# TensorE's wait for the scaled key copies moved from ahead of the key-key products to between them and the key-query products

## What is computed

```
qkvz = x @ W_qkvz.T                       # per key head: q, k, 2 v, 2 z of 128
q, k, v = silu(conv4(q)), silu(conv4(k)), silu(conv4(v))
q, k = rmsnorm(q), rmsnorm(k)             # sums of squares of q and k
decay[c, m] = exp(g[c] - g[m])            # c >= m, g a running sum
T = inverse(I + strict_lower(beta * (k k^T) * decay))
attn = (q k^T) * decay                    # key-query products
for each chunk:                           # the state carries over
    v_new = T (beta v) - T (beta k exp(g)) state
    out = (q exp(g)) state + attn v_new
    state = state * exp(g_last) + (k * exp(g_last - g))^T v_new
out = rmsnorm(out) * silu(z) @ W_out.T
```

## Time and profile before

| what | value |
|---|---|
| median of 3 runs | 3789.3 us |
| the profiled execution | 3785.71 us, its span 3783.8 us |
| TensorE matmul busy | 88% of the span |
| TensorE weight load busy | 69% |
| VectorE, ScalarE, GpSimd busy | 65%, 52%, 40% |
| mean granted TensorE clock | 0.982 |

### The profile page before, as it was taken

How to read it: one execution, slowest core, us unless ns; L and a number is a source line. 1 busy time by engine, 2 the same in 40 slices (tenths; PEclk the granted TensorE clock), 3 DMA queues, 4 the chain that set the end, 5 groups by cost and what they waited for, 6 DMA issues and landing times. The chain is left out here.

```text
span 3783.8 us, 58251 instructions
## 1 busy us (share of the span) xinstructions
PE 3344.6 (88%) x18978; PEld 2619.3 (69%) x18978; DVE 2453.1 (65%) x5143; ACT 1968.5 (52%) x4746; POOL 1505.5 (40%) x2617
## 2 busy tenths in 40 slices
PE   0114999999999999999999999999999999999987
PEld 0113777777777777777777777777777777777763
DVE  6873566666666666666676666666666666666643
ACT  5762555554555555555555555555555555555531
POOL 9963343433433343434344333434333433334310
PEclk9998999999999999999999999999999999999988
DMA  2013222222222222222222222222222122222202
GB/s 95 33 50 135 70 73 73 72 54 71 75 74 64 67 62 76 75 75 69 53 70 77 72 68 72 54 76 76 73 75 70 51 78 70 74 66 66 56 5 100
DMA packets 291213, 261.53 MB, mean 69 GB/s; under 512 B 220992, under 2 KB 249792, under 8 KB 281152
## 3 DMA queue, kind: packets, MB, share of 16 engines
q1 hardware_dynamic: 281696, 123.60, 13.5%
q10 hardware_dynamic: 9216, 134.22, 9.6%
HBM read 228.11 MB, written 29.62 MB: 68 GB/s over the span
## 5 line engine op out<-in xcount | busy, mean ns | idle before, releaser
L638 PE MATMUL x<-xs,w_high 128*128 128x512 f32 x3072 | 1063.4, 427 | 40.0 <-POOL w_low L1229 34.6
L638 PE MATMUL x<-xs,w_low 128*128 128x512 f32 x1536 | 613.6, 399 | 0.0
L873 ACT ACTIVATE uvec<-rb,cpos 128x128 f32<-128x128 f32 x512 | 160.1, 364 | 868.5 <-PE rb L658 868.5
L638 PEld LDWEIGHTS x<-xs,w_high 128*128 128x128 f32 x3072 | 531.3, 193 | 104.5 <-POOL w_low L1229 35.5
L937 ACT ACTIVATE slot<-lane 128x512 fp32r<-128x512 f32 x640 | 350.8, 608 | 402.1 <-PE lane L764 401.7
L1212 POOL TENSOR_TENSOR block_step<-block_in 64x14 f32<-64x14 f32 (+6 forms) x896 | 229.1, 256 | 506.3 <-DMA block_in<-blocks_dram 385.6
L1244 POOL TENSOR_TENSOR rstd<-rarg,powers 128x8 f32<-128x8 f32 x64 | 105.4, 1647 | 625.8 <-DVE rarg L1046 625.8
L638 PEld LDWEIGHTS x<-xs,w_low 128*128 128x128 f32 x1536 | 292.4, 190 | 67.8
L764 PEld LDWEIGHTS lane<-pinv,slot 128*128 128x128 f32 x1536 | 200.2, 192 | 190.2 <-ACT slot L937 98.9
L1009 DVE SCALAR_TENSOR_TENSOR cacc<-x,cwqk,cacc 128x511 f32<-128x511 f32 (+2 forms) x384 | 281.2, 746 | 44.3 <-ACT cacc L860 22.4
L1009 DVE SCALAR_TENSOR_TENSOR cacc<-x,cwv,cacc 128x511 f32<-128x511 f32 (+2 forms) x384 | 281.7, 747 | 37.9 <-ACT cacc L860 4.1
(11 more groups left out here) (203 smaller groups left out, 7737.2 us busy)
## 6 DMA issues: line engine op xcount, KB each, us to landing
xs<-mix_dram ACTq DMA_DIRECT2D x64, 2048.0 KB, 7.7
gb<-cum_dram SPq DMA_DIRECT2D x128, 256.0 KB, 4.4
w_in<-in_w_qkvz SPq DMA_DIRECT2D x48, 512.0 KB, 4.1
w_out<-in_w_out SPq DMA_DIRECT2D x16, 512.0 KB, 4.7
blocks_dram<-bt SPq DMA_DIRECT2D x512, 8.0 KB, 1.5
inverse_dram<-block_out SPq DMA_DIRECT2D x64, 128.0 KB, 2.2
inv<-inverse_dram SPq DMA_DIRECT2D x512, 16.0 KB, 1.8
side_kv<-in_side SPq DMA_DIRECT2D x4, 1024.0 KB, 11.5
```

Source lines behind the costliest of these rows:

```text
L638: ins = mm(PROJ_BANK[kind][i][:, :], w, x, start=(k == 0 and j == 0), stop=(k == KC - 1 and j == 2))
L873: ins = a(uvec[:, h, :], rb[:, sl(h, HD)], ACT.Copy, scale=sm2[p]["cpos"][:, ch, h:h + 1])
```

## The change

The wait on `ktok_ready` is no longer issued ahead of both groups of matmuls but in the loop, ahead of the second group:

```diff
             def key_products(l, m, p):
                 W("qk_ready", 2 * l + 2)
-                if m is not None:
-                    W("ktok_ready", m + 1)
                 for i, bank, name in ((0, x0, "kk_full"), (1, rc, "kq_products_full")):
+                    if i == 1 and m is not None:
+                        W("ktok_ready", m + 1)
                     for ch in range(NCH):
                         ins = mm(bank[:, sl(ch, CH)], qkT2[p][:, 0, sl(ch, CH)], qkT2[p][:, i, sl(ch, CH)], start=True, stop=True)
                     ins.then_inc(S[name], 1)
```

## The result

| | before | after |
|---|---|---|
| median | 3788.6 us (4 runs, 3787.47 to 3796.2) | 3871.1 us (4 runs, 3860.16 to 3878.43) |
| ratio to before | | 1.0211, 95% interval 1.0182 to 1.0240 |
| profiled execution, span | 3785.71, 3783.8 us | 3860.16, 3858.4 us |
| mean granted TensorE clock | 0.982 | 0.958 |

The account below looks back on a forecast made before the run. TensorE, busy 88% of the span, was taken to bound the kernel. 112 us of clock falls, less 16 us paid now and 8 us gained, gave +88 us: 3874 us profiled, 3877 us median, range 3785 to 3960.

Parts of the forecast that it names:

- The old stall: TensorE's key-key products wait for ScalarE's scaled key copies; claimed to go, about 0.7 us in each of 62 iterations.
- What is late next: One-column sums wait for ScalarE's squares; only 0.13 us an iteration gained, 8 us in all, about 0.55 us left idle.
- The clock: TensorE's granted clock in the loop: low stretches in 45 iterations instead of 11, 2.5 us each, 112 us.
- a fifth longer: Idle time's lengthening of TensorE's one-column matmuls and transposes, the ground for taking 45 iterations with a clock fall.
- The lean stretch: TensorE's one-column sums, then transposes; claimed to grow from 2.6 to some 3.1 us with idle time, lowering the clock.
- my first rival: TensorE's clock as now or with fewer falls, gain as worked out: 3781 us, or 3771; chance 0.12.
- The full stall: Rival: the sums do not wait for the squares, so 62 x 0.7 = 43 us go, 3746 us; chance 0.03.
- The trace sides with the second: Claim that the profile favours the skill's short-idle-times section, since the clock falls with no idle gap at all.

Follow-up runs that it names:

- e2: Changed kernel plus one-column repeats of two key-key products in the idle time ahead of the sums; 3884.3 us, 1.0248 to the kernel before.
- e1: Changed kernel with two of the four key-key products repeated at full width right ahead of the one-column sums; 3855.3 us, 1.0166 to the kernel before.
- e8: Changed kernel with one 128-column product of the recurrence done twice per iteration, far from the sums; 3867.3 us, 1.0215 to the kernel before.
- e9: e1 with one 128-column product of the recurrence done twice per iteration, far from the sums; 3806.1 us, 1.0037 to the kernel before.
- e4: Changed kernel with a quarter of the z projection moved from behind the third product step to ahead of the sums; 3754.1 us, 0.9907 to the kernel before.
- e6: e4 with the last quarter of the z projection moved between the sums and the transposes; 3754.5 us, 0.9909 to the kernel before.

## Why the prediction was right, and where its reasons fell short

Forecast 3877 us, measured 3871.1 us, and slower was given 0.79.

- **The old stall, 0.7 us.** Right: the key-key products follow the projection after 0.23 us and the moved wait costs nothing.
- **What is late next.** Right. The sums wait for the squares 61 times from 420 to 3640 us. I took 0.13 us of gain an iteration, from a release time between 0.05 and 0.11 us; the release took 0.05 us (1220.09 to 1220.14) and the gain is 0.16 us, 10 us in all for my 8. The idle time is 0.59 us for my 0.55.
- **The clock.** Right in sign, place and size. 49 falls for my 45; 2.1 us each (101 us / 49) for my 2.5. A long fall costs 3.2 us, above the 2.9 I had as the most. Falls among the transposes and low stretches of double length came as described, and the mean clock is 0.958 for "about 0.95". That the sum comes so near (112 us forecast for all falls, 101 measured) is in part luck: I took too few falls at too high a price, and the 45 came from "a fifth longer", which doesn't lead to the 39 falls of a kernel without that idle time.
- **The reason for the clock: the step that falls short.** "The lean stretch grows from 2.6 us to some 3.1 us" is true and counts (e2 against e1, e8 against e9), but I made it the sole cause. With full work in the idle time 39 falls are left (e1). The other cause goes with the very gain of the change: the iteration is 0.16 us shorter. At 51.37 us and no idle time there 39 falls, at 51.58 us 17. My sum contained no term for it, and my first rival, "clock as now" if the idle time does no harm, would have failed at that too.
- **The rivals.** The full stall was not gained: the squares hold the sums. It is gained once they are covered (e4). The rule of the Trainium skill's "TensorE: Matmul & The Clock Gate" ("Why this matters for your kernels"), that only long idle gaps lower the clock in mid-kernel, is not borne out: here it falls in 39 of 61 iterations of a kernel with none near it (e1). Its section "A second HAM failure mode: psum-queue depth-cycling", a clock that oscillates by short idle times, fits the changed kernel but not e1, where there are none near the falls, nor the kernel before, whose TensorE was busy for 6.04 of 6.05 us ahead of one. "The trace sides with the second" was too much: a fall with no idle time agrees with neither.

Why the length of an iteration matters can be read from the kept traces. In each of the twelve, all changes of the granted clock (33 in the kernel before, 117 in the changed one) lie on one evenly spaced row of times, to within 0.001 us, whatever the loop does. So I sorted the iterations by how long after their key-key products the first time of that row comes; a fall begins at a later time of the same row:

| | iterations with a fall | iterations without |
|---|---|---|
| before | 2.54 to 2.79 us | 0.09 to 1.01, 2.85 to 3.39 |
| e1 | 1.52 to 2.09, 3.01 to 3.38 | 0.03 to 1.36 |
| e9 | 1.41 to 2.56, 3.08 to 3.32 | 0.02 to 1.36, 2.58 to 2.94 |

In each of these kernels that one time settles whether an iteration has a fall. e1 and e9, alike around the sums, don't contradict each other anywhere and differ in how often they come to the places of a fall. A fall lengthens its iteration and so moves the next one: in e1 an iteration of 52.88 us with the row's time at 3.24 is followed by one at 1.56, which falls too; in e9 one of 53.10 us at 3.18 is followed by one at 1.28, which doesn't. So in e1 34 of 38 falls are followed by a fall in the very next iteration, in e9 5 of 17, in the changed kernel 46 of 48, in the kernel before none of 11. Nearly all the falls that the change added are such followers. The part of the idle time shows as well: where the row's time comes at 0.98 to 1.37 us, e8 falls in all of 21 iterations and e9, with full work in place of the idle time, in none of 14. Why just these places bring a fall stays open.

## What to carry to other kernels

A wait moved to where it is needed gains only what the next wait on the same queue leaves, and moves the idle time next to other work: find cover for that next wait in the same edit (here one projection quarter turned +82 us into -35 us). Where the granted clock falls now and then after a stretch of one-column matmuls and transposes, count those falls before and after any change, even one that only shortens the loop, and look whether they come singly or one behind the other. A full matmul inside such a stretch can lower their number (e6: 3), if nothing needs it elsewhere.

## What the runs showed that I had not expected

The time of this kernel is not monotone in its work: e9 does one product of 0.2 us more in each iteration than e1 and is 49 us faster. And with no idle time near them, sums and transposes of 2.6 us went with a lower clock in 11 (before), 17 (e9) or 39 (e1) of 61 iterations; between the last two stands nothing but one product far from the sums, 0.2 us of iteration length.
